# Gated cross-attention with feed-forward on one core: weighted values ahead of the turned rows, and the seams of the three parts reordered

## What is computed

```python
def layer_norm(x, g, b): ...          # over the last axis
def attention(x, kv):                 # x is already normalised once
    q = layer_norm(x, g_x, b_x) @ w_q                    # 16 heads of 32
    k, v = split(layer_norm(kv, g_kv, b_kv) @ w_kv)
    p = softmax(where(mask == 0, -1e9, q @ k.T * 32**-0.5))
    return (p @ v) @ w_proj + b_proj
def ffn(x):
    w1, w2 = (q - 128) * scales ...                      # 512 x 2048, 2048 x 512
    return x + 0.5 * (silu(layer_norm(x, g, b) @ w1 + b1) @ w2 + b2)
x = x + tanh(g_xattn) * attention(layernorm(x), ctx)
x = x + tanh(g_ffn) * ffn(layernorm(x))
```

## Time and profile before

| | before |
|---|---|
| runs, us | 1099.16, 1098.69, 1100.47 (median 1099.16) |
| the profiled execution | 1100.38 us, span 1098.6 us |
| PE / DVE / ACT / POOL busy, share of the span | 94% / 60% / 36% / 30% |
| granted TensorE clock, mean | 0.984 of 2.4 GHz |
| attention's steady part, 130 to 370 us: PE busy | 232.99 of 239.78 us |
| end of attention, 370 to 413.8 us: PE busy | 31.47 of 43.78 us |
| first chunk of the feed-forward, 413.8 to 501.4 us: PE busy, DVE busy | 83.98, 69.85 of 87.60 us |
| rest of the feed-forward: PE busy | 593.56 of 597.23 us |

### The profile page before, as it was taken

How to read it: one execution, slowest core, us unless ns; L and a number is a source line. 1 busy time by engine, 2 the same in 40 slices (tenths; PEclk the granted TensorE clock), 3 DMA queues, 4 the chain that set the end, 5 groups by cost and what they waited for, 6 DMA issues and landing times.

```text
span 1098.6 us, 15131 instructions
## 1 busy us (share of the span) xinstructions
PE 1031.2 (94%) x5182; PEld 561.0 (51%) x5182; DVE 654.2 (60%) x1071; ACT 398.9 (36%) x612; POOL 329.7 (30%) x338
## 2 busy tenths in 40 slices
PE   5767899999999878999999999999999999999998
PEld 3444567767766553444444444444444444444443
DVE  5677898898887767786435335345345335335322
ACT  3455777777776633331121121121121121121111
POOL 3554577667575442202102102102102002012000
PEclk9888999999999999999999999999999999999999
DMA  8574677678775668602001001100100200200101
GB/s 275 135 190 127 184 203 215 200 202 239 196 200 164 188 194 288 229 1 77 1 1 65 13 1 40 37 1 35 45 1 3 74 1 1 77 1 1 39 1 39
DMA packets 61473, 109.38 MB, mean 100 GB/s; under 512 B 9656, under 2 KB 10848, under 8 KB 60896
## 3 DMA queue, kind: packets, MB, share of 16 engines
q1 hardware_dynamic: 58632, 104.11, 31.0%
q10 hardware_dynamic: 2776, 4.40, 1.4%
HBM read 72.57 MB, written 33.55 MB: 97 GB/s over the span
## 4 chain that ended last, share of the span: by engine, by line
PE 61%; DVE 1%; issue 0%; ACT 0%; DVEq 0%
PE ps_z L1406 10%; PE ps_z L1408 10%; PE ps_z L1407 10%; PE ps_y L238 10%; PE ps_y L239 10%; PE ps_y L240 10%; PE ps_h L1420 1%; DVE x_in L1528 0%; DVE x L1490 0%; DVE y_hi L1467 0%; DVE w_lo L195 0%; DVE w_f L192 0%; ACT w_hi L183 0%; DVEq L1296 0%; DVE y_lo L1469 0%
## 5 line engine op out<-in xcount | busy, mean ns | idle before, releaser
L1441 ACT ACTIVATE y_f<-ps_y,cols,ffn_scales 128x512 f32<-128x512 f32 x128 | 99.3, 776 | 489.9 <-PE ps_y L240 489.9
L1467 DVE TENSOR_SCALAR y_hi<-y_f,ffn_scales 128x512 f16<-128x512 f32 x128 | 70.1, 548 | 330.3 <-ACT y_f L1441 330.3
L1406 PE MATMUL ps_z<-w_hi,y_hi 128*128 128x512 f16 x512 | 194.8, 380 | 3.6 <-DVE w_lo L195 3.6
L238 PE MATMUL ps_y<-ht_hi,w_hi 128*128 128x512 f16 x512 | 194.6, 380 | 1.6 <-PEq L278 1.5
L1408 PE MATMUL ps_z<-w_hi,y_lo 128*128 128x512 f16 x512 | 194.8, 381 | 0.0
L1407 PE MATMUL ps_z<-w_lo,y_hi 128*128 128x512 f16 x512 | 194.8, 381 | 0.0
L239 PE MATMUL ps_y<-ht_lo,w_hi 128*128 128x512 f16 x512 | 194.6, 380 | 0.0
L240 PE MATMUL ps_y<-ht_hi,w_lo 128*128 128x512 f16 x512 | 194.4, 380 | 0.0
L1469 DVE SCALAR_TENSOR_TENSOR y_lo<-y_f,ffn_scales,y_hi 128x512 f16<-128x512 f32 x128 | 103.2, 806 | 4.6
L761 ACT ACTIVATE p_f<-ps_s,fill_col 128x512 f32<-128x512 f32 x128 | 86.2, 674 | 6.3 <-PE ps_s L592 6.3
L763 ACT ACTIVATE p_hi<-ps_s,fill_col 128x512 f16<-128x512 f32 x128 | 85.4, 667 | 0.0
(11 more groups left out here) (201 smaller groups left out, 1585.5 us busy)
## 6 DMA issues: line engine op xcount, KB each, us to landing
q_pack<-q_dram SPq DMA_DIRECT2D x96, 256.0 KB, 4.0
q_dram<-q_hi SPq DMA_DIRECT2D x32, 256.0 KB, 3.5
q_dram<-q_lo SPq DMA_DIRECT2D x32, 256.0 KB, 4.3
x_dram<-x_out SPq DMA_DIRECT2D x32, 256.0 KB, 4.8
x_res<-in_x SPq DMA_DIRECT2D x30, 256.0 KB, 4.6
q_raw<-in_L_ffn_fc_q SPq DMA_DIRECT2D x6, 1024.0 KB, 9.3
s_raw<-in_L_ffn_fc_scales SPq DMA_DIRECT2D x6, 1024.0 KB, 12.4
x_in<-in_x SPq DMA_DIRECT2D x4, 1024.0 KB, 8.8
```

The lines of the kernel that those rows point to most:

```text
L238: nc.tensor.matmul(out, s_hi, m_hi, start=(k == 0), stop=False)
L1406: nc.tensor.matmul(ps_z[t][:, :], hi, w2_hi[:, f, :], start=(f == 0), stop=False)
L1441: nc.scalar.activation(y_f[f % 2][:, :], ps_y[f % 2][:, :], ACT.Silu, bias=b1_c[:, f:f + 1], scale=y_unscale).then_inc(y_f_ready, 1)
L1467: nc.vector.tensor_scalar(y_hi[f % 4][:, :], y_f[f % 2][:, :], y_scale, None, ALU.mult).then_inc(y_hi_ready, 1)
```

## The change

1. In PE's step `weighted_values` of unit k-1 comes before `turn_x`, not behind it, so that `turn_x` and `turn_maxima` follow one another.
2. Start of attention: in step -1 ACT takes the maxima of unit 0 before the queries and rows; SP packs them before it stores the queries of unit 1, and loads the rows of chunk 2 at the end of that step instead of a step earlier; DVE does `row_stats(0, 2)` behind p_lo of unit 0, and the five small groups of `numbers` behind the maxima of their step instead of ahead of them.
3. End of attention: the residual rows of the last four tiles (before: two) have buffers of their own: p_f0 and p_f1, loaded in step 32 when the last p_lo are made, and xt_f0 and xt_f1.
4. Feed-forward: weight slice (1, 0) is made in step -2 instead of step 0, and the base of chunk 0 (DVE and POOL) in step 3 instead of step -2.

```diff
+        def last_tiles(i, k):
+            return isinstance(i, int) and PER * i + k >= UNITS - KB
+
+        last_res = [p_f[0][:, :], p_f[1][:, :], xt_f[0][:, :], xt_f[1][:, :]]
 
         def residual(i, k):
-            return xt_f[k % 2][:, :] if last_pair(i, k) else x_res[k % 2][:, :]
+            return last_res[k % KB] if last_tiles(i, k) else x_res[k % 2][:, :]
...
+            def load_last(t):
+                sp.dma_start(last_res[t], x_tiles[(NCHUNK - 1) % 2, (NCHUNK - 1) // 2, t, :, :]).then_inc(last_res_loaded[t], 16)
+
             def step(i, k):
...
-                if k % KB == 2:
+                if k % KB == 2 and k != -2:
                     load_x(i, k // KB + 3)
...
                     sp.wait_ge(xt_lo_ready, UNITS + KB)
-                    for n in range(2):
-                        sp.dma_start(xt_f[n][:, :], x_tiles[(NCHUNK - 1) % 2, (NCHUNK - 1) // 2, KB - 2 + n, :, :]
-                                     ).then_inc(last_res_loaded[n], 16)
-                if real(i, tile, UNITS) and not last_pair(i, tile):
+                    load_last(2)
+                    load_last(3)
+                if isinstance(i, int) and PER * i + k == UNITS:
+                    sp.wait_ge(p_lo_dve, lo_counts(0, UNITS - 1)[0])
+                    load_last(0)
+                    load_last(1)
+                if real(i, tile, UNITS) and not last_tiles(i, tile):
...
+                if k == -1:
+                    pack_maxima(i, k + 1)
                 if real(i, k + 2, UNITS):
                     store_queries(i, k + 2)
-                if real(i, k + 1, UNITS):
+                if real(i, k + 1, UNITS) and k != -1:
                     pack_maxima(i, k + 1)
+                if k == -1:
+                    load_x(i, 2)
...
                 if real(i, k + 2, UNITS):
                     queries(i, k + 2, second)
+                if real(i, k - 1, UNITS):
+                    weighted_values(i, k - 1)
                 if real(i, k + AHEAD, UNITS + KB):
                     turn_x(i, k + AHEAD)
-                if real(i, k - 1, UNITS):
-                    weighted_values(i, k - 1)
                 if real(i, k + 1, UNITS):
                     turn_maxima(i, k + 1)
...
             def step(i, k):
+                first_maxima = isinstance(i, int) and PER * i + k == -1
+                if first_maxima:
+                    take_maxima(i, k + 1)
                 if real(i, k + 2, UNITS):
                     take_queries(i, k + 2)
                 if real(i, k + AHEAD, UNITS + KB):
                     take_x(i, k + AHEAD)
-                if real(i, k + 1, UNITS):
+                if real(i, k + 1, UNITS) and not first_maxima:
                     take_maxima(i, k + 1)
...
-                    if half == 1:
-                        row_stats(0, 2) if k == 0 else normalise_rows(0, 2)
+                    if half == 1 and k == 1:
+                        normalise_rows(0, 2)
                     return
...
                 rows_in_step(i, k, 0)
+                if isinstance(i, int) and PER * i + k in numbers:
+                    numbers[PER * i + k]()
                 if real(i, k + 2, UNITS):
                     queries_lo(i, k + 2)
...
                     probabilities_lo(i, k, 1)
+                if isinstance(i, int) and PER * i + k == 0:
+                    row_stats(0, 2)
...
+            numbers = {2: weight_scales, 3: hidden_bound, 4: hidden_scales, 5: row_gain, 6: row_shift}
...
+        FIRST_BASE = 3
...
             def step(i, k):
+                if isinstance(i, int) and i == 0 and k == -2:
+                    weights_hi(act, *w_steps[0])
...
-                if isinstance(i, int) and i == 0 and k in w_steps and k >= 0:
+                if isinstance(i, int) and i == 0 and k in w_steps and k > 0:
                     weights_hi(act, *w_steps[k])
...
+            def base(i, c):
+
+                chunk, b = 2 * i + c + 1, (c + 1) % 2
+                for t in range(TT):
+                    after(dve, norm_ready, TT * (chunk - 1) + t + 1)
+                    nc.vector.scalar_tensor_tensor(out=x1[b][:, t, :], in0=x1_norm[:, t, :], scalar=u_scale[:, t:t + 1],
+                                                   in1=x1[b][:, t, :], op0=ALU.mult, op1=ALU.add).then_inc(sum_ready, 1)
+
             def step(i, k):
                 c, f = k // FB, k % FB
+                if isinstance(i, int) and i == 0 and k == -2:
+                    weights(dve, *w_steps[0])
...
+                if isinstance(i, int) and i == 0 and k == FIRST_BASE:
+                    base(i, -1)
...
+            def add_bias(i, c):
+
+                chunk, b = 2 * i + c + 1, (c + 1) % 2
+                for t in range(TT):
+                    after(pool, sum_ready, TT * chunk + t + 1)
+                    nc.gpsimd.tensor_tensor(x1[b][:, t, :], x1[b][:, t, :], b2_rows[:, :], ALU.add).then_inc(base_ready, 1)
```

More of the change, by code:

```diff
@@ L353, in attention @@
         res_loaded = [sem("res_loaded0"), sem("res_loaded1")]
-        last_res_loaded = [sem(f"last_res_loaded{n}") for n in range(2)]
+        last_res_loaded = [sem(f"last_res_loaded{n}") for n in range(KB)]
         q_stored, q_packed, max_packed = ([sem(f"{name}{n}") for n in range(2)] for name in ("q_stored", "q_packed", "max_packed"))
@@ L1129, in last_steps @@
                     g("weights")(dve, 0, (u - UNITS) // 2)
+            numbers = {2: weight_scales, 3: hidden_bound, 4: hidden_scales, 5: row_gain, 6: row_shift}
             every_step(dve, step, {-8: context_rows, -7: lambda: [masks(), scale_maxima()], -4: lambda: [key_parts(), row_stats(0, 1), key_means()], -1: lambda: [value_bound(), scale_maximum()],
-                              0: value_scale, 2: weight_scales, 3: hidden_bound, 4: hidden_scales, 5: row_gain, 6: row_shift})
+                              0: value_scale})
         @block.gpsimd
@@ L1523, in step @@
                     split_h(i, c + 1, f - TURN)
-                if f == BASE:
-                    for t in range(TT):
-                        after(dve, norm_ready, TT * (chunk - 1) + t + 1)
-                        nc.vector.scalar_tensor_tensor(out=x1[b][:, t, :], in0=x1_norm[:, t, :], scalar=u_scale[:, t:t + 1],
-                                                       in1=x1[b][:, t, :], op0=ALU.mult, op1=ALU.add).then_inc(sum_ready, 1)
+                if f == BASE and k >= 0:
+                    base(i, c)
             every_step(dve, step)
@@ L1534, in _ @@
         def _(pool):
+            def add_bias(i, c):
[3 more added lines that the diff above has]
+                    nc.gpsimd.tensor_tensor(x1[b][:, t, :], x1[b][:, t, :], b2_rows[:, :], ALU.add).then_inc(base_ready, 1)
             def step(i, k):
                 c, f = k // FB, k % FB
+                if isinstance(i, int) and i == 0 and k == FIRST_BASE:
+                    add_bias(i, -1)
                 if not real(i, FB * (c + 1)):
@@ L1560, in step @@
                     nc.gpsimd.tensor_tensor(ln_r[:, :], ln_r1[:, :], ln_r2[:, :], ALU.mult).then_inc(scales_ready, 1)
-                if f == BASE:
-                    for t in range(TT):
-                        after(pool, sum_ready, TT * chunk + t + 1)
-                        nc.gpsimd.tensor_tensor(x1[b][:, t, :], x1[b][:, t, :], b2_rows[:, :], ALU.add).then_inc(base_ready, 1)
+                if f == BASE and k >= 0:
+                    add_bias(i, c)
             every_step(pool, step)
```

7 lines of the change are left out of this document (2 added, 5 removed).

## The result

The kernel after takes 1125.52 us in the median of three runs (1125.08 to 1130.76) against 1099.16: slower by 2.6%, a ratio of 1.0258 over all runs with an interval of 1.0235 to 1.0280 (the two medians alone give 2.4%). In a second series of five rounds it stood at 1.0249 (1.0235 to 1.0263). The forecast was 1116.5 and slower: the direction and the mechanism of the steady units came out as written, the size was 9 us too small. The stated range ended at 1126; the ratio puts the kernel at 1127.5, outside it, and the median just inside. The profiled execution was the longest of the three, 1130.76 us with a span of 1128.9 and a mean clock of 0.974; the other two had spans of 1123.3 and 1123.7 at 0.983.

What follows compares the result with a forecast made beforehand. ACT's queue, nearly level with PE, was taken to bound each attention unit. Start -5.2, units +23.3, projections' end -4.3, first hidden chunk +3.5 summed to +17.3 us: 1116.5 us, range 1107 to 1126.

Steps and rivals of the forecast that it cites:

- The reordered unit: Steady attention units: ACT's two row copies stand before max_row, third score at Q (queries' end) +5.01, not +4.13: +0.88 us each.
- Late units: Five units (k = 8, 12, 16, 20, 24) whose weighted values wait for POOL's p_lo: +1.50 us each, bounds 1.35 and 1.75.
- The start: Units up to 5: fewer waits for maxima and less half clock, less the units' growth: -5.2 us (-8 to -1).
- Rival (c): Attention units: PE's longer waits lower the granted clock, five falls give +9 us, 1125.5; chance 0.07.
- The end of the projections: Earlier residual loads remove PE's 2.46 us wait for x_out and about 1.8 of half clock: -4.3 us (-3.5 to -5).
- The first hidden chunk: Feed-forward: the 3.62 us wait for w2's first slice goes, but base in step 3 makes later slices late: +3.5 us.
- (a): First hidden chunk: base is absorbed, -4.2 us in place of +3.5, 1108.8; chance 0.15.
- (d): Attention units: ACT's stretch is not lengthened, units keep their time, the other changes give -6.0 us, 1093; chance 0.07.
- (e): Units grow by a fifth of the forecast and the other changes cancel it: no change; chance 0.03.
- (b): Start of attention gains nothing: the 1 MB load lands late and half clock stays, +5.2 us, 1121.7; chance 0.12.

Runs made afterwards that it cites:

- short copies: The kernel after, but ACT's two row copies (xt_hi, xt_f) take only 128 of 512 columns from job 8 on: ratio 1.0140 to before, 1118.35 us.
- the seams alone: The kernel after with PE's old order (turn_x ahead of weighted_values), all other parts of the change kept: ratio 0.9950 to before, 1093.93 us.
- the filler: The kernel after with score 1 of units 0 to 4 issued seven times more on PE: ratio 1.0228 to before, 1124.23 us.
- rows and scales later: Before with items 2 and 3, the last group's normalisations behind o_f and POOL's row scales behind its p_lo: ratio 1.0116 to before, 1111.48 us.
- the best kernel: After with PE's old order, base in step 0, two last-group normalisations and POOL's bias_residual moved later in step 25: 0.9899; with four score repeats 0.9868.
- order and small groups: Before with PE's new order and the five small groups behind the maxima, nothing else: ratio 1.0262 to before, 1127.51 us.

## Why the prediction was right in kind and wrong in size

**The reordered unit: right.** "max_row stands behind both in ACT's queue" is what the rows show, the short copies prove it one for one, and the 0.88 taken was 1.03 in the mean of the 17 units that are neither late nor unit 26 (17.5 us in all). With Q = 221.83 in unit 14 (221.60 and one product of 0.23) the third score is at Q+5.17, against 5.01: the weighted values begin at Q+0.10 as worked out, and what is over lies at xt_hi, which follows the first turn by 0.70 or 0.78, against 0.64. The projection's six products, held up by xt_f, end level with p_hi: they start 0.05 behind it and the first takes 0.33, without which the prediction's six of 0.23 behind Q+3.36 would have ended at Q+4.74 and not at its Q+5.0. Of the Trainium skill's rule on tiling modes (TensorEngine Tiling (Array Packing), Key Properties) the trace shows no more than before: the turn starts 0.32 behind the last weighted group in both orders. By that rule alone the unit kept its time; it grew by 1.

**Late units: mis-sized,** 1.50 taken, 2.14 measured in the mean. The chain was right (xt_lo behind a later xt_f); of the piece missed, 0.64, some 0.4 lies on POOL, in its first row-scale operation (0.21 us before, 0.65 in after). Together with the steady units: 28.2 us in 22 units, where the prediction's terms give 22.5. Unit 26 gave 3.6 back, which no term had; that the stage's sum came within 1.4 us of the forecast (2.6 like for like) is luck, two errors of opposite sign.

**The start: the step that failed.** "Sum 0.5+4.3+2.0-1.7+0.1 = 5.2" priced the waits for maxima of the earlier trace rows as a gain and took the order's 0.88 off in four units. The runs show that the longer units alone make DVE's maxima timely (0.6 us of waits in place of 7.3), and that moving the small groups then gives nothing (1.0262 against 1.0270), while it gives 0.4% with the old order. It also took full clock for units 2 and 3; the start of after had 30.7 us at half clock, where before had 13.7. The size of the failed step, profile against profile: the order was priced at 4 x 0.88 = 3.5 us in this stage, and after reaches the third score of unit 6 10.0 us later than the seams alone (136.76 against 126.76); unit 0 stands 1.17 later, and units 1 to 6 take 0.97, 2.10, 2.12, 1.75, 0.92 and 0.99 longer. Rival (c) had the mechanism of the clock, but argued it from the steady units, where the projection fills most of PE's wait and the clock stayed at 1.00. In the profiles it came in the units that have no projection.

The start is 7.6 of the 13.1 us by which the profiled sum was off. The profile overstates it: the medians were off by 9.0. After and the seams alone differ by 35.7 us in span in their profiles, and by 1.0249 to 1.0258 less 0.9950, 32.9 to 33.9 us, in the ratios; if all of that difference lies in the start, the order cost 7 to 8 us there (an estimate), still twice what was taken. No profile of such an execution shows it. How much of it is the clock stays open: the filler took 17 us of half clock away and brought some 5 us in its profile, 1 to 2 in the medians.

**The end of the projections: half.** The wait of 2.46 for x_out is gone, as forecast; the 1.8 of clock did not come: 10.2 us of that stage are at half clock, 6.8 before. -1.7 measured (-2.9 without unit 30), -4.3 taken.

**The first hidden chunk: right place, lower size.** Base costs DVE 6.6 us, as worked out (6.4), PE waits at a slice of w2, and the clock falls in that wait: +5.1, inside the bound of +6 that was given for just this, where +3.5 was taken. The third wait came at the turned rows of the next chunk and not at slice (1, 6).

**Rivals.** (a) base absorbed, (d) ACT's stretch unchanged and (e) no change are excluded. (b), that the start gains nothing, came true at its time of 1121.7 plus the errors above, by another road than the late 1 MB load. The range's upper end of 1126 held one cause at a time; (b) and (c) together, 5.2 and 9 us, would have given 1130.7. That the median of 1125.52 is the number of (c) alone is chance: (c) had five falls of the clock in units and the seams' full gain.

## What to carry to other kernels

An order on one engine is also an order on the engines that serve it: before moving a step, lay the in-order queue of every consumer beside it and see what now stands in front of the short operation on the critical path. Waits that two edits both remove can be gained once only, so price a bundle of edits in the schedule that the others leave behind, not in the old trace. And where a pipeline is not yet full, look for waits that nothing fills: behind such waits the start of after ran at half clock for 30.7 us.

## What the runs showed of the hardware

- **Some operations of DVE and POOL hold each other up for whole instructions.** A normalisation (128x512 f32, SBUF to SBUF) takes 0.54 us alone and 1.51 to 1.53 beside a POOL addition of 1.4 (1.37 to 1.50 in the rows and scales later); a pair of splits 1.3 alone and 3.1 beside POOL's bias adds. Not all do: the transposes into inv_den (L906 of after) take 0.71 us in the 18 units where they run beside a POOL operation and in the 14 where they don't. The Trainium skill (SBUF — State Buffer, SBUF: two separate sides) says that the two engines share one pair of ports, which is locked for a whole instruction of GpSimd or of certain kinds of DVE operation. The trace agrees: in before two normalisations fit in front of xt_lo, and each of the other two lasts about as long as one of POOL's additions (1.37 and 1.47).
- **More PE work raised the granted clock.** 35 repeated matmuls in the first five units went with a granted clock of 0.90 in place of 0.77 between 65 and 125 us, and the mean clocks of the five executions are 0.983 to 0.989, those of the eight of after 0.974 to 0.983. In the profile unit 6 came some 5 us earlier; the medians moved by 1 to 2 us, inside the noise. With 20 of them the best kernel went from 0.9899 to 0.9868, with intervals that just touch. Why the clock fell there was not settled: before had a longer single wait in the same stretch (4.4 us) and a higher clock, 0.92, and with waits cut to 1.61 us in three of the five units the short copies still had 0.80.
- **The start differs from one execution to the next.** The same code had the third score of unit 6 at 134.34 and at 131.51. Executions of after at a mean clock of 0.982 to 0.983 had spans of 1121.8 to 1125.4, those at 0.974 and 0.975 had 1128.9 and 1128.1. All four profiles of the full new order are of the second kind; of the 14 executions of these kernels without a profile two are, at 0.974 (order and small groups), and a third at 0.977 stands between, so what was read above of the start's clock holds for that kind alone. A mean of 0.983 means some 20 us less at half clock than 0.974 (38 against 58 us, an estimate from spans and mean clocks).
